# Cross-attention and mixture-of-experts block on one core: the last layernorm with two-tile statistics and accumulating stores

## What is computed

```python
res = hidden_states + combined.reshape(B, S, D)
mu = jnp.mean(res, -1, keepdims=True)
var = jnp.var(res, -1, keepdims=True)
return (res - mu) * jax.lax.rsqrt(var + 1e-05) * ln_gamma + ln_beta
...
x = x + _L0_ffn_ref(_layernorm(x, axis=-1), ...)
```

## Time and profile before

| what | us |
|---|---|
| median of 3 runs (lowest, highest) | 767.0 (766.27, 769.16) |
| profiled execution: span, first to last instruction | 769.2 |
| its own time (the page gives none but the span) | 769.2 |
| last stage, landing of the last scatter to the end | 728.0 to 769.2 |

### The profile page before, as it was taken

One profiled execution on the slowest core, in us unless ns is written; L12 is line 12 of the kernel. 1 busy time (PEld: TensorE's weight loads), 2 busy tenths in 40 slices (PEclk: granted clock), 3 DMA queues, 4 the chain that ended last, 5 costly groups with the idle time before them and its releaser, 6 DMA issues.

```text
span 769.2 us, 15696 instructions
## 1 busy us (share of the span) xinstructions
PE 680.1 (88%) x5592; PEld 649.1 (84%) x5592; DVE 564.4 (73%) x1198; ACT 406.3 (53%) x955; POOL 430.1 (56%) x547
## 2 busy tenths in 40 slices
PE   5999999999999834999999999999999999999500
PEld 4789999998988723999999999999999999999500
DVE  5589898988888797665565679777696666854187
ACT  3356555555555594454454467455464454643185
POOL 6744665565564334436445558766576554632456
PEclk9699999999999955999999999999999999999855
DMA  9501101011010122434344446544455343322484
GB/s 295 176 15 43 42 28 43 30 41 43 29 43 29 42 85 65 149 84 94 51 107 69 81 106 123 125 96 73 98 123 114 46 101 52 58 29 28 64 266 150
DMA packets 55764, 64.10 MB, mean 83 GB/s; under 512 B 9472, under 2 KB 50944, under 8 KB 55552
## 3 DMA queue, kind: packets, MB, share of 16 engines
q0 software_dynamic: 15360, 21.31, 17.1%
q1 hardware_dynamic: 39616, 41.64, 16.6%
q10 hardware_dynamic: 704, 0.01, 0.0%
HBM read 39.22 MB, written 23.72 MB: 82 GB/s over the span
## 4 chain that ended last, share of the span: by engine, by line
PE 81%; DVE 11%; issue 3%; DMA 2%; ACT 1%; POOL 1%; POOLq 0%; SPq 0%; DVEq 0%; ACTq 0%
PE banks L897 18%; PE banks L899 18%; PE banks L898 18%; PE banks L1039 8%; PE banks L1025 5%; PE banks L1013 5%; PE banks L1171 2%; PE banks L1075 1%; PE banks L920 1%; DVE oh_lo L1485 1%; PE banks L942 1%; DVE oh_id L1481 1%; DVE z L1741 1%; DMA res<-sum_rows 1%; DVE z L1735 1%
## 5 line engine op out<-in xcount | busy, mean ns | idle before, releaser
L611 POOL DMA_INDIRECT sum_rows<-y_sb,slot_ids x80 | 131.4, 1643 | 162.1 <-ACT y_sb L840 145.4
L850 ACT ACTIVATE hraw<-banks,b_now 128x256 f32<-128x256 f32 x320 | 132.2, 477 | 90.3 <-PE banks L899 80.5
L897 PE MATMUL banks<-xT_hi,w_hi 128*128 128x256 f32 x560 | 161.6, 289 | 1.7 <-ACT xT_hi L822 1.7
L899 PE MATMUL banks<-xT_hi,w_lo 128*128 128x256 f32 x560 | 158.5, 283 | 0.0
L898 PE MATMUL banks<-xT_lo,w_hi 128*128 128x256 f32 x560 | 158.4, 283 | 0.0
L897 PE MATMUL banks<-w_hi,h_hi 128*128 128x256 f32 x528 | 148.8, 282 | 1.3 <-issue 1.3
L898 PE MATMUL banks<-w_lo,h_hi 128*128 128x256 f32 x528 | 148.6, 281 | 0.0
L899 PE MATMUL banks<-w_hi,h_lo 128*128 128x256 f32 x528 | 148.5, 281 | 0.0
L1701 DVE TENSOR_TENSOR h_lo<-hraw,h_hi 128x512 fp32r<-128x512 f32 x160 | 114.6, 716 | 5.5
L1699 DVE CAST h_hi<-hraw 128x512 fp32r<-128x512 f32 x160 | 77.5, 485 | 45.8 <-ACT hraw L850 44.6
L897 PEld LDWEIGHTS banks<-xT_hi,w_hi 128*128 128x128 f32 x560 | 106.3, 190 | 2.2 <-issue 2.1
(11 more groups left out here) (216 smaller groups left out, 1442.7 us busy)
## 6 DMA issues: line engine op xcount, KB each, us to landing
w1raw<-in_w1T SPq DMA_DIRECT2D x8, 1024.0 KB
w2raw<-in_w SPq DMA_DIRECT2D x8, 1024.0 KB
xn_rows<-xn SPq DMA_DIRECT2D x32, 128.0 KB, 1.8
sum_rows<-xn SPq DMA_DIRECT2D x32, 128.0 KB, 1.8
out<-z SPq DMA_DIRECT2D x16, 256.0 KB, 2.2
res<-sum_rows SPq DMA_DIRECT2D x7, 512.0 KB, 8.5
X<-in_x SPq DMA_DIRECT2D x2, 1280.0 KB, 12.1
xg<-xn_rows,slot_ids POOLq DMA_INDIRECT x80
```

The costliest lines, as they stand in the source:

```text
L611: g.indirect_dma_start(sum_rows, bass.IndirectOffsetOnAxis(ap=slot_ids[:, st, 1, q:q + 1], axis=0), y_sb[:, u, q, :], None, bounds_check=N ...
L850: a.activation(hraw[:, j // 2, j % 2, :], banks[:, j // 2, (j % 2) * 256:(j % 2 + 1) * 256], ACT.Silu, bias=b1_now[:, (c // SPE) % 2, j:j ...
L897: t_.matmul(o, a_hi, b_hi, start=first, stop=False)
L899: return t_.matmul(o, a_lo, b_hi, start=False, stop=last)
```

## The change

The statistics of two tiles are made by one `bn_stats` over 512 elements in the order tile 0, tile 1, tile 0, tile 1, so that the even half is one tile and the odd half the other; no aggregation follows. DVE makes `(res - mean) * (16 gamma)` for the first three tiles of a quad and ACT multiplies them by the power; the last tile of a quad goes to ACT and then to POOL. The sum of squared deviations is not divided by D = 256: the power is 1/16 of the reciprocal standard deviation, and `gamma_16` holds 16 gamma. `X` (x + beta) is stored to the output during the expert stage, by eight plain stores from SP. The results of the last stage are stored by sixteen DMAs from POOL that add to what the output holds.

```diff
+            act.wait_ge(load_gb, 32)
+            a.activation(gamma_16[:], gamma_sb[:], ACT.Copy, scale=16.0).then_inc(sem("gamma_made"), 1)
...
                 sp.dma_start(w2raw[:], w2[ds(e, 1)].rearrange("a (j p) d -> p (a j) d", p=P)).then_inc(load_w2, 16)
+                sp.wait_ge(sem("beta_added"), QT * e)
+                sp.dma_start(out_t[:, ds(QT * (e - 1), QT), :], X[:, ds(QT * (e - 1), QT), 0:D]).then_inc(based, 16)
+            sp.wait_ge(sem("beta_added"), NT)
+            sp.dma_start(out_t[:, NT - QT:NT, :], X[:, NT - QT:NT, 0:D]).then_inc(based, 16)
...
-            for g, a in enumerate(halves_in_order()):
-                sp.wait_ge(sem("out_made"), g + 1)
-                sp.dma_start(out_t[:, a:a + 2, :], z[:, a:a + 2, :]).then_inc(stored, 16)
...
+            pool.wait_ge(based, 16 * NQ)
+            def deviations(k):
                 if k < NQ:
+                    pool.wait_ge(sem("var3_made"), k + 1)
                     quad = slice(QT * k, QT * (k + 1))
...
+            deviations(0)
+            for k in range(NQ):
+                a, last = QT * k, QT * (k + 1) - 1
+                deviations(k + 1)
+                pool.wait_ge(sem("rows_scaled"), (QT - 1) * k + 2)
+                g.dma_start(out_t[:, a:a + 2, :], z[:, a:a + 2, :], accum_op=ALU.add).then_inc(stored, 16)
+                pool.wait_ge(sem("last_scaled"), k + 1)
+                g.tensor_tensor(z[:, last, :], z[:, last, :], gamma_16[:], ALU.mult).then_inc(sem("z_scaled"), 1)
+                pool.wait_ge(sem("rows_scaled"), (QT - 1) * (k + 1))
+                pool.wait_ge(sem("z_scaled"), k + 1)
+                g.dma_start(out_t[:, a + 2:a + 4, :], z[:, a + 2:a + 4, :], accum_op=ALU.add).then_inc(stored, 16)
...
+            for k in range(NQ + 1):
                 if k < NQ:
...
+                    act.wait_ge(sem("rstd3_made"), k + 1)
+                    for n in range(QT - 1):
+                        t = QT * k + n
+                        act.wait_ge(sem("z_made"), (QT - 1) * k + n + 1)
+                        a.activation(z[:, t, :], z[:, t, :], ACT.Copy, scale=rstd_d[:, t:t + 1])                            .then_inc(sem("rows_scaled"), 1)
+                if k >= 1:
+                    t = QT * k - 1
+                    act.wait_ge(sem("nmr_made"), k)
                     a.activation(z[:, t, :], res[:, t, :], ACT.Identity, scale=rstd_d[:, t:t + 1],
-                                 bias=nmr_d[:, t:t + 1]).then_inc(sem("z_made"), 1)
+                                 bias=nmr_d[:, t:t + 1]).then_inc(sem("last_scaled"), 1)
...
+            def pair_stats(n):
+                v.bn_stats(st_d[:, n].rearrange("p a b -> p (a b)"), res[:, 2 * n:2 * n + 2, :].rearrange("p t d -> p d t"))\
+                    .then_inc(sem("st3_made"), 1)
+
+            def centred(t):
+                v.scalar_tensor_tensor(z[:, t, :], res[:, t, :], st_d[:, t // 2, t % 2, 1:2], gamma_16[:],
+                                       ALU.subtract, ALU.mult).then_inc(sem("z_made"), 1)
...
+                    for n in range(2):
+                        res_loaded(dve, a0 + 2 * n)
+                        pair_stats(2 * k + n)
...
+                    v.tensor_scalar_add(var_d[:, a0:a0 + QT].rearrange("p (a b) -> p a b", b=2),
+                                        st_d[:, 2 * k:2 * k + 2, :, 2], D * EPS_LN).then_inc(sem("var3_made"), 1)
+                    centred(a0 + 1)
+                    centred(a0 + 2)
+                if k >= 1:
                     dve.wait_ge(sem("rstd3_made"), k)
```

More of the change, by code:

```diff
@@ L207, in xattn_moe_kernel @@
         z = sb("z", [P, NT, D], f32, C)
[L208 to L212, removed]
-        C.close()
[L215 to L221, removed]
+        st_d = sb("st_d", [P, NT // 2, 2, 3], f32, C)
+        var_d = sb("var_d", [P, NT], f32, C)
+        rstd_d, nmr_d = sb("rstd_d", [P, NT], f32, C), sb("nmr_d", [P, NT], f32, C)
+        gamma_16 = sb("gamma_16", [P, D], f32, C)
+        C.close()
         banks = root.enter_context(nc.psum_tensor("banks", [P, 8, 512], f32))
@@ L238, in xattn_moe_kernel @@
             "key_rows_made kT_made w_hi_ready v_hi_made xn1T_hi_made q_hi_made pT_made probs_made valsT_hi_made wg_made parts_made router_exp row_made lo_apart lo_made_act "
-            "xT_hi_made h_made y_scaled w_hi_made z_made mean16_made act_stats_made "
+            "xT_hi_made h_made y_scaled w_hi_made gamma_made rows_scaled last_scaled "
             "kT_done v_done v_rows_done xn1T_done q_done scores_done pT_done pv_done valsT_done out_done "
@@ L246, in xattn_moe_kernel @@
             "var2_made router_shifted second_made sel_made routed tokens_counted early_located located scale_made hi_made lo_made ids_made xT_lo_made "
-            "h_hi_made h_lo_made y_made st3_made mv3_made var3_made nmr_made z_scaled_dve out_made"
+            "h_hi_made h_lo_made y_made st3_made var3_made nmr_made z_made"
         ).split():
@@ L266, in xattn_moe_kernel @@
         load_res = [dma_sem(f"load_res{n}") for n in range(len(RES_LOADS))]
-        stored = dma_sem("stored")
+        based, stored = dma_sem("based"), dma_sem("stored")
         block = root.enter_context(nc.Block())
@@ L651, in _ @@
                     g.tensor_tensor(X[:, st, 0:D], X[:, st, 0:D], beta_sb[:], ALU.add).then_inc(sem("beta_added"), 1)
-            for k in range(NQ + 1):
+            pool.wait_ge(based, 16 * NQ)
+            def deviations(k):
                 if k < NQ:
+                    pool.wait_ge(sem("var3_made"), k + 1)
                     quad = slice(QT * k, QT * (k + 1))
[L657 to L663, removed]
+                    g.tensor_tensor(rstd_d[:, quad], var_d[:, quad], minus_half[:, 0:QT], ALU.pow)                        .then_inc(sem("rstd3_made"), 1)
+            deviations(0)
[9 more added lines that the diff above has]
+                g.dma_start(out_t[:, a + 2:a + 4, :], z[:, a + 2:a + 4, :], accum_op=ALU.add).then_inc(stored, 16)
         @block.scalar
@@ L858, in _ @@
             expert_steps(act, expert_step)
-            def first_two(k):
+            act.wait_ge(load_gb, 32)
+            a.activation(gamma_16[:], gamma_sb[:], ACT.Copy, scale=16.0).then_inc(sem("gamma_made"), 1)
+            for k in range(NQ + 1):
                 if k < NQ:
[L864 to L886, removed]
+                    act.wait_ge(sem("rstd3_made"), k + 1)
@@ L1715, in _ @@
             expert_steps(dve, expert_step)
-            dve.wait_ge(sem("beta_added"), NT)
-            for k in range(NQ + 2):
-                first, last = slice(QT * k, QT * k + 2), slice(QT * k + 2, QT * (k + 1))
-                if k < NQ:
[L1723 to L1738, removed]
-                    dve.wait_ge(sem("rstd3_made"), k)
[L1740 to L1747, removed]
@@ new lines, in pair_stats @@
+            def pair_stats(n):
[4 more added lines that the diff above has]
+                                       ALU.subtract, ALU.mult).then_inc(sem("z_made"), 1)
+            for k in range(NQ + 1):
+                a0, last = QT * k, QT * k - 1
+                if k < NQ:
+                    for n in range(2):
+                        res_loaded(dve, a0 + 2 * n)
+                        pair_stats(2 * k + n)
+                    dve.wait_ge(sem("st3_made"), 2 * k + 1)
+                    if k == 0:
+                        dve.wait_ge(sem("gamma_made"), 1)
+                    centred(a0)
+                    dve.wait_ge(sem("st3_made"), 2 * k + 2)
+                    v.tensor_scalar_add(var_d[:, a0:a0 + QT].rearrange("p (a b) -> p a b", b=2),
[3 more added lines that the diff above has]
+                if k >= 1:
+                    dve.wait_ge(sem("rstd3_made"), k)
+                    v.scalar_tensor_tensor(nmr_d[:, last:last + 1], st_d[:, last // 2, 1, 1:2], -1.0, rstd_d[:, last:last + 1],
+                                           ALU.mult, ALU.mult).then_inc(sem("nmr_made"), 1)
```

## The result

The changed kernel takes 785.0 us (median of 4 runs, 783.63 to 785.82), the kernel before 767.2 (4 runs, 766.27 to 769.16): a ratio of 1.0233, 95% interval 1.0217 to 1.0249. The forecast was 783.4 us. The profiled execution of the changed kernel took 783.63 us, its span is 781.9; every run has about 1.7 us outside its span. By that, the profiled execution of before took about 770.9 us and was a long one: the 769.2 given above as its own time is its span.

The account below looks back on a forecast made before the run. POOL was to bound the last stage at 5.73 us a quad: 736.8 + 40.1 + 4.3 + 3.1 + 1.3 = 785.6 us, carried to the median 783.4, 2.1% slower; 781 to 792 us for g from 1.3 to 2.2, chance 0.43.

Parts of the forecast that it names:

- The dear end of the bounds: DVE, last stage: a 512-wide statistic at 1.5 us if the alternating order doubles it, making DVE's quad 4.8 us.
- The early stores: SP's queue, expert stage: eight 512 KB stores of the residual, covered by an expert's matmuls; counted as nothing.
- The wait is over before it is reached: SP's queue: the early store's wait for POOL's additions ends before SP gets there, so the next weight load isn't held.
- POOL's sum: Last stage, one quad on POOL: power, ACT's chain, multiplication, step to the store and second store; 5.73 us against 3.54 before.
- The price g: Time for which one accumulating store holds POOL in the last stage; taken as 1.58 us, the scatter's row.
- The argument for 1.58: POOL's store priced like the 128-row accumulating scatter: the list saved is set against the rows added.
- Rival 2: POOL's stores: every row is paid, g 2.6 us gives 798 us, 3.16 gives 807; chance 0.20.
- Rival 1: POOL's stores are cheap: g 1.08 us, the gather's, gives 779 us; SP's 0.37 gives 772.5; chance 0.27.
- Rival 3: No change: command writing lies beside POOL's work, g = 0, a quad 4.15 us, total 769 us; chance 0.06.
- The DMA engines: Last stage: a 256 KB accumulating store takes 1.7 us, under POOL's 2.9 us between stores; transfers end at 768.6, before POOL.
- The sum: Last stage: quad 1's power at 736.8, seven quads 40.1, last quad 4.3, landing 3.1, end 1.3: 785.6 us.
- From the last landing to the end 1.3 us: Program end: time from the last store's landing to the end of the span, 1.3 us, from the profile before.

Follow-up runs that it names:

- the run with the early stores alone: Kernel before, with the residual stored early by SP and overwritten by the last stores; nothing else changed: 766.8 us, ratio 1.0000.
- half and half: Against before: paired statistics, ACT's last tile in the same quad, first pairs by POOL adding stores except last two quads, the rest plainly by SP: 761.7 us.
- The run with SP's stores: Changed kernel with both stores of a quad issued by SP as plain stores, residual left out of the sum: 766.8 us, ratio to before 1.0001.
- the run with ACT's order: Changed kernel, but ACT makes a quad's last tile right behind its three scalings, not behind those of the next quad: 778.8 us.
- the run without the multiplication: Changed kernel with the fourth tile centred on DVE and scaled on ACT like the others; POOL has only power and two stores: 772.7 us.
- without adding: Changed kernel with POOL's stores not accumulating, so the output lacks the residual: 779.7 us, ratio to before 1.0158.

## Why the prediction was right

The time is 1.6 us over the forecast. Its steps, in their order:

- **The bound.** POOL leads the chain and DVE idles: as forecast.
- **The statistics.** Priced at 0.75 us, 0.69 measured. The dear end of the bounds, 1.5, did not come. Of the two statements of the Trainium skill, "Vector Engine (DVE) Microarchitecture Reference", on the SBUF access granule, the second holds here: one stream that alternates between two regions runs at full rate; 0.691 us for 512 columns is below the estimate of 0.96 from its other rate, and below the 0.75 of two contiguous operations.
- **The early stores.** Their price, nothing, was right, and the step "The wait is over before it is reached" was wrong: I paired the store with the weight load of the wrong expert. In the changed kernel SP waited there 115.0 us in five waits, the longest 41.4. That it costs nothing rests on the other half of the step, the cover by the matmuls, and the run with the early stores alone shows it.
- **POOL's sum.** Forecast 1.18 + 1.95 + 0.86 + 0.16 + 1.58 = 5.73; measured 1.07 + 1.93 + 0.93 + 0.55 + 1.20 = 5.68 from single rows, 5.65 from start to start. Two terms were mis-sized by 0.4 us, one up and one down, and they cancel; that is luck. The price g is 1.20, between the gather's 1.08 and the scatter's 1.58. The step from multiplication to store is 0.55 and not 0.16: the 0.16 came from a gather that does not read what the addition before it wrote, while the store waits for POOL's own result. In half and half, where it doesn't wait for it, the gap is gone.
- **The two ways to price g.** The argument for 1.58, the list saved against the rows added, doesn't hold: rows are 0.12 us for 256, the adding is 0.47 a store, the rest 0.73. Rival 2 (every row paid) falls. The forecast's own condition, g from 1.3 to 2.2, was missed too: with 1.20 and everything else as it was, its sum gives 780.0. Rival 1 had the price nearly right (1.08), but by the same sum would have forecast 779, because it shared the 0.16. The Trainium skill, "DMA: Bandwidth & Descriptors", Anatomy of one DMA, says that many descriptors can be emitted before the added cost shows. The trace agrees: 1.32 against 1.20 us for twice the rows.
- **Rival 3's floor.** With g = 0 a quad was put at 4.15. The run with SP's stores shows 3.86 in the mean and no gain, so in this order of work no price of the store could have made one.
- **The DMA engines.** 1.7 us for a store, hidden under POOL's pace: right, as the run with ACT's order shows, whose quads are shorter with the same stores. In the run without the multiplication the engines took a store every 1.75 us and were then 1.4 us further behind POOL at the end, so the 1.7 is about their limit; by itself it was not measured.
- **The sum.** Forecast from the landing to the first chained power 8.8 us, seven quads 40.1, last quad 4.3, end 4.4, together 57.6; measured 7.7, 39.2, 3.8, 6.9, together 57.7. The last term is the one that failed: "From the last landing to the end 1.3 us" was read off a kernel whose last stores came from SP. Behind POOL's stores it is 3.2 us to the end of POOL's drain, and 3.5 to the end of the span. The terms before it were too long by 1.1, 0.9 and 0.5 us, and the last too short by 2.5: the bound and its chain were forecast, but that the sum meets to 0.1 us is luck.
- **From the profiled execution to the median.** Of the 17.8 us between the medians, the two profiles show 16.4 in the stage of the table; that of before was about a microsecond long, as the kernel with the early stores alone, whose last stage has the same program, shows with 43.8.

## What to carry to other kernels

Work taken off the bound engine is a gain only up to the next engine's pace: write out the next engine's whole quad, in program order and with its turns through other engines, before moving anything to it. An adding store replaces an addition only where the engine that issues it has about 1.2 us free per store, and a program that ends on such stores ends later: 6.9 us passed here from POOL's last work to the end, against 3.6 from DVE's last work before. Sixteen of them made the kernel slower; six stood in a version that was faster, whose other changes no run takes apart from them. And fewer, larger stores do not help when the one that is saved had been waiting beside something else.

## What the runs showed of the hardware that was not expected

- **POOL's end.** In the five kernels whose last stores came from POOL, its drain ended 2.9 to 3.4 us after SP had seen the last landing (781.6 against 778.4 with the change, 778.6 against 775.2 without adding). In the kernels that store from SP alone it ended 1.0 to 1.1 us after it, and in half and half, whose last adding store lay 9 us before the end, 0.1 us before it. What the drain waits for, the traces do not show.
- **The packets of an adding store take three times as long as a plain one's:** by the DMA share 4.5 against 1.5 us of the engines' time a quad. That is not the time that the engines need, since packets overlap: without the multiplication on POOL two adding stores went through in 3.49 us.
- **A neighbour's price.** DVE's two centrings take 0.87 us as a rule and 1.34 where POOL's multiplication runs beside them (DVE's row at 740.45, POOL's multiplication from 740.59 to 741.51), and the multiplication 0.92 there and 0.72 alone. In the run without the multiplication the three centrings in a row take 1.26 to 1.27 us in every quad and none is stretched, so the stretch goes with POOL's multiplication. The other half, the multiplication's 0.72 and 0.92, is read from rows alone.
